# Attention in a four-layer kernel: the order of three matmul groups in a round, the sum of the weights on one engine, the division in four parts

## The chip, the cores and the metric

The kernel runs on one NeuronCore of a Trainium2 chip. The engines that matter here are TensorE (PE in the profile; PEld is its weight load), VectorE (DVE), ScalarE (ACT) and GpSimd (POOL). Matmuls write to PSUM, eight banks of 512 float32 columns on 128 partitions; GpSimd works on SBUF only. The metric is the device time of one execution in microseconds, and the median of the runs is what counts.

## The reference, cut to what matters

Four layers, each followed by a residual sum and a layer norm, on 2048 tokens of 128 numbers: a test-time-training attention, an 8-expert feed-forward layer, a softmax attention, and a gated 8-expert layer. The change is in the third:

```python
q = (x @ Wq).reshape(b, s, 16, 64)      # s = 2048 tokens, 16 heads of 64
k = (x @ Wk).reshape(b, s, 16, 64)
v = (x @ Wv).reshape(b, s, 16, 64)
dot = jnp.einsum('bihd,bkhd->bhik', q, k)
w = jax.nn.softmax(dot / 8, axis=-1)
a = jnp.einsum('bhij,bjhd->bihd', w, v).reshape(b, s, 1024)
return a @ Wo + bo
```

## The kernel before, in words

The attention goes through 32 units. A unit U is a pair of heads (p = U // 4) and 512 queries (U % 4); head h of the pair lies on rows 64h to 64h+63 of every operand. A unit has 8 rounds (d = 0 to 7, R = 8U + d), and a round covers two steps, that is two blocks of 128 keys. There are 256 rounds.

What TensorE does in one round, in the order of its queue (loop at L1827):

1. **late maximum** (`maximum`, L1734 to L1742, matmuls at L1740): two matmuls, one for each head, with 64 rows each, into banks 5 and 6. They are rough scores of unit U+1 (U+2 from d = 7 on), of 128 queries against 512 keys, and serve only to find each query's maximum. DVE reduces the two banks (L1945) and gives them back through the semaphore `free5`. There is no second pair of banks for this.
2. **the negated maxima** (L1758 to L1760): four matmuls with 32 rows each that write minus the maximum into the four score banks 0 to 3. They wait until ACT has taken the exponentials of the round before (L1757).
3. **scores** (L1761 to L1767): twelve matmuls with 64 rows, two by two (six pairs), added to the same four banks.
4. **early maximum** (L1740 again): like the late one, for the next 128 queries. It waits at L1699 until DVE has given banks 5 and 6 back after the late one.
5. at most one **misc job** in bank 7 (`misc_job`, L1568): keys at d = 0, the output product of unit U-2 at d = 1, the sum of the weights of U-1 over the partitions at d = 2, values at d = 3, queries at d = 4, the negated maxima turned by a matmul (`mask`, L1744) at d = 7.
6. **weigh** (L1769 to L1783): eight matmuls with 128 rows and 64 columns, the values times the exponentials of the round before, into bank 4.

ACT takes two exponentials a round (L1883, 128x1024 each), written to eight buffers `Pb`. The sum over the keys is kept in `acc`: `acc += Pb` for 15 of a unit's 16 steps, columns 0 to 831 on GpSimd (L2077) and 832 to 1023 on DVE (L1996). ACT reuses a buffer when weigh and both adds of eight steps ago are done.

DVE's queue in a round (L2024 to L2043): reduce of the late maximum, `negate` at d = 7 (L1947, two small reduces after all maxima of the next unit), the two adds of the round before, reduce of the early maximum, its part of the misc job, one quarter of the reciprocal of the sum at d = 3 to 6 (`invert`, L1968), and at d = 7 the product of reciprocal and head output (`normalise`, L1976, 128x512).

Semaphores order all of this; the queues are written out by hand and `Plan` (L1593) only numbers the uses of each bank.

Of the kernel before, what the change touches and what calls it, by code (L numbers as in the profile page):

```python
# [16 lines left out]
P = 128  # L17
# [52 lines left out]
NT = 16  # L70
# [1488 lines left out]
RN = NT // 2  # L1559
ROUNDS = UNITS * RN  # L1560
STEPS = 2 * ROUNDS
POOL = 832
BUFS = 8
SCALE = 1.0 / float(np.sqrt(D))
B_O, B_M, B_P = 4, 5, 7
# [2 lines left out]
def misc_job(R):  # L1568

    U, d = R // RN, R % RN  # L1570
    p, qt = U // NU, U % NU
    if d == 0 and p < PAIRS - 1:
        return "k", p + 1, qt
    if d == 1 and U > 1:
        return "out", U - 2
    if d == 2 and U:
        return "sum", U - 1
    if d == 3 and p // 2 < PAIRS // 2 - 1:
        return "v", p // 2 + 1, U % RN
    if d == 4 and U < UNITS - 2:  # L1580
        return "q", U + 2
    if d == 7 and U < UNITS - 1:
        return "mask", U + 1
    return None
# [107 lines left out]
def attention_pe(k):  # L1692
# [12 lines left out]
    def freed(key):  # L1705
        bank, n = plan.at[key]
        pe.wait_ge(S[f"free{bank}"], n)
# [38 lines left out]
        bank = begin(("mask", U))  # L1746
        end(pe.matmul(ps[:, bank, 0:P], b.nm[:, :], k.ident[:, :], start=True, stop=True), bank)

    def scores(R):
        U, d = R // RN, R % RN  # L1750
        p = U // NU
        if d == 0:
            freed(("mask", U))
            freed(("q", U))
            freed(("k", p, NU - 1))
        if R:
            pe.wait_ge(S["probs"], 2 * R)  # L1757
        for g in range(4):  # L1758
            rows = slice(32 * g, 32 * (g + 1))
            pe.matmul(ps[:, 2 * (g % 2) + g // 2, :], b.ones[rows, :], b.Mr[rows, :], start=True, stop=False, tile_position=(32 * g, 0))  # L1760
        for i in range(2):  # L1761
            kc, slot = 2 * d + i, 2 * i
            at = slice(kc * P, (kc + 1) * P)
            for n, (K, Q) in enumerate(((b.Kh, b.Qh), (b.Kh, b.Ql), (b.Kl, b.Qh))):
                for h in range(2):
                    last = pe.matmul(ps[:, slot + h, :], K[HEAD[h], p % 2, at], Q[HEAD[h], U % 3, :], start=False, stop=(n == 2))  # L1766
            last.then_inc(S["scores"], 1)  # L1767
# [15 lines left out]
            last.then_inc(S["weighted"], 1)  # L1783

    def sums(U):
        pe.wait_ge(S["added_dve"], 15 * (U + 1))
        pe.wait_ge(S["added_pool"], 15 * (U + 1))
        bank = begin(("sum", U))
        for h in range(2):
            last = pe.matmul(ps[HEAD[h], bank, :], k.ones[:, 0:D], b.acc[:, U % 2, h * QT:(h + 1) * QT], start=True, stop=True)  # L1790
        end(last, bank)

    def output(U):
        pe.wait_ge(S["normalised"], U + 1)
        bank = begin(("out", U))
        end(pe.matmul(ps[:, bank, :], k.att_o[:, U // NU, :], b.On[:, :], start=True, stop=True), bank)  # L1796

# [28 lines left out]
    pe.wait_ge(S["att_wo"], 16)  # L1826
    for R in range(ROUNDS):  # L1827
        late, early = max_jobs(R - 1)[1], max_jobs(R)[0]
        if R and late:
            maximum(*late[1:])  # L1830
        scores(R)
        if early:
            maximum(*early[1:])
        if misc_job(R):
            misc(misc_job(R))
        if R:
            weigh(R - 1)
# [11 lines left out]
def attention_act(k):  # L1849
    b, S, ps, act = k.a, k.S, k.ps, k.nc.scalar  # L1850
    plan = b.plan

    def begin(key):
        bank, n = plan.at[key]
        act.wait_ge(S[f"full{bank}"], n)
        return bank

    def queries(U):
        bank = begin(("q", U))
        act.activation(b.Qh[:, U % 3, :], ps[:, bank, :], ACT.Copy).then_inc(S["high"], 1)  # L1860

    def keys(p, qt):
        bank = begin(("k", p, qt))
        act.activation(b.Kh[:, p % 2, qt * QT:(qt + 1) * QT], ps[:, bank, :], ACT.Copy).then_inc(S["high"], 1)

    def values(G, j):
        bank = begin(("v", G, j))
        act.activation(b.Vb[:, G % 2, 2 * j:2 * j + 2, :].rearrange("p a d -> p (a d)"), ps[:, bank, :], ACT.Copy).then_inc(S[f"free{bank}"], 1)

    def sums(U):  # L1870
        bank = begin(("sum", U))
        if U:
            act.wait_ge(S["inverted"], 4 * U)
        act.activation(b.ssum[:, :], ps[:, bank, :], ACT.Copy).then_inc(S[f"free{bank}"], 1)  # L1874

    def probs(step):
        slot = 2 * (step % 2)
        act.wait_ge(S["scores"], step + 1)
        if step >= BUFS:
            act.wait_ge(S["weighted"], step - BUFS + 1)  # L1880
            act.wait_ge(S["added_dve"], adds_of(step - BUFS))
            act.wait_ge(S["added_pool"], adds_of(step - BUFS))
        act.activation(b.Pb[:, step % BUFS, :], ps[:, slot:slot + 2, :].rearrange("p a b -> p (a b)"), ACT.Exp, scale=SCALE).then_inc(S["probs"], 1)  # L1883

    def heads_out(U):
        act.wait_ge(S["weighted"], NT * (U + 1))
        if U > 1:
            act.wait_ge(S["normalised"], U - 1)
        act.activation(b.Or[:, U % 2, :], ps[:, B_O, :], ACT.Copy).then_inc(S["heads_out"], 1)

    act.wait_ge(S["tile_y0"], 16 * (SLOTS_T // 2))
    act.wait_ge(S["tile_y1"], 16 * (SLOTS_T // 2))
    act.activation(b.ones[:, :], k.ones[:, :], ACT.Copy)
    gather_norm_act(k, 1)
    for g in range(NU):
        bank = begin(("x", g))
        act.activation(b.xh[:, g * QT:(g + 1) * QT], ps[:, bank, :], ACT.Copy).then_inc(S["high"], 1)
    queries(0)
    for qt in range(NU):
        keys(0, qt)  # L1900
    queries(1)
    for j in range(RN):
        values(0, j)
    for R in range(ROUNDS):
        U, d = R // RN, R % RN
        probs(2 * R)
        probs(2 * R + 1)
        key = misc_job(R)
        if key and key[0] in "qkv":
            {"q": queries, "k": keys, "v": values}[key[0]](*key[1:])  # L1910
        if key and key[0] == "sum":
            sums(U - 1)
        if d == 0 and U:
            heads_out(U - 1)
    heads_out(UNITS - 1)
    sums(UNITS - 1)
    for g in range(4):
        norm_act(k, 8 + g, g)


def attention_dve(k):
# [20 lines left out]
    def maximum(U, m):  # L1942
        quarter, qc = m // 4, m % 4
        bank = begin(("max", U, m))
        v.tensor_reduce(b.mx[:, :, qc, quarter:quarter + 1], ps[:, bank:bank + 2, :], AX.X, ALU.max).then_inc(S[f"free{bank}"], 1)  # L1945

    def negate(U):  # L1947
# [14 lines left out]
                        ALU.mult).then_inc(S[f"free{bank}"], 1)  # L1962

    def invert(U, part):
        bank, n = plan.at["sum", U]
        v.wait_ge(S[f"free{bank}"], n)
        at = slice(part * P, (part + 1) * P)
        v.reciprocal(b.rec[:, at], b.ssum[:, at]).then_inc(S["inverted"], 1)  # L1968

    def normalise(U):  # L1970
        v.wait_ge(S["inverted"], 4 * U + 4)
        v.wait_ge(S["heads_out"], U + 1)
        if U:
            bank, n = plan.at["out", U - 1]
            v.wait_ge(S[f"full{bank}"], n)
        v.tensor_tensor(b.On[:, :], b.rec[:, :], b.Or[:, U % 2, :], ALU.mult).then_inc(S["normalised"], 1)  # L1976

    def output(U):
        qt = U % NU
# [2 lines left out]
            v.wait_ge(S[f"free{bank}"], plan.at["out", U - NU][1])  # L1982
        yq = k.y_all[:, 4 * qt:4 * qt + 4, :]
        v.tensor_tensor(yq, ps[:, bank, :].rearrange("p (a d) -> p a d", a=4), yq, ALU.add).then_inc(S[f"free{bank}"], 1)

    def add(step):
        U, kc = step // NT, step % NT
        u, at = U % 2, slice(POOL, 2 * QT)
        v.wait_ge(S["probs"], step + 1)
        if kc > 1:  # L1990
            v.wait_ge(S["added_dve"], adds_of(step - 1))
        elif U > 1:
            bank, n = plan.at["sum", U - 2]
            v.wait_ge(S[f"full{bank}"], n)
        before = b.Pb[:, (step - 1) % BUFS, at] if kc == 1 else b.acc[:, u, at]
        v.tensor_tensor(b.acc[:, u, at], before, b.Pb[:, step % BUFS, at], ALU.add).then_inc(S["added_dve"], 1)  # L1996

    v.wait_ge(S["tile_y0"], 16 * (SLOTS_T // 2))
    v.wait_ge(S["tile_y1"], 16 * (SLOTS_T // 2))
# [24 lines left out]
    for R in range(ROUNDS):  # L2024
# [3 lines left out]
            maximum(*late[1:])  # L2028
        if d == 7 and U < UNITS - 1:
            negate(U + 1)  # L2030
        if R:
            if (R - 1) % RN:
                add(2 * R - 2)
            add(2 * R - 1)
        if early:
            maximum(*early[1:])
        key = misc_job(R)
        if key and key[0] in ("q", "k", "mask", "out"):
            {"q": queries, "k": keys, "mask": mask, "out": output}[key[0]](*key[1:])
        if U and 3 <= d <= 6:  # L2040
            invert(U - 1, d - 3)
        if U and d == 7:
            normalise(U - 1)  # L2043
    for step in (STEPS - 2, STEPS - 1):
        add(step)
    output(UNITS - 2)
    for part in range(4):
        invert(UNITS - 1, part)
    normalise(UNITS - 1)
    output(UNITS - 1)  # L2050


# [10 lines left out]
def attention_pool(k):  # L2063
# [2 lines left out]

    def add(step):
        U, kc = step // NT, step % NT
        u, at = U % 2, slice(0, POOL)
        g.wait_ge(S["probs"], step + 1)  # L2070
        if kc == 1 and U > 1:
            bank, n = plan.at["sum", U - 2]
            g.wait_ge(S[f"full{bank}"], n)
        if step > 1:
            g.wait_ge(S["added_pool"], adds_of(step - 1) if kc > 1 else 15 * U)
        before = b.Pb[:, (step - 1) % BUFS, at] if kc == 1 else b.acc[:, u, at]
        g.tensor_tensor(b.acc[:, u, at], before, b.Pb[:, step % BUFS, at], ALU.add).then_inc(S["added_pool"], 1)  # L2077

    for step in range(STEPS):
        if step % NT:  # L2080
# [78 lines left out]
```

## Time and profile before

| | us |
|---|---|
| three timed runs | 1982.34, 1986.2, 1986.29 |
| median | 1986.2 |
| the profiled execution | 1982.01 |
| its span, first to last instruction | 1980.3 |
| attention rounds in it | from 474.4 to about 1786 |
| PE busy | 1745.4 (88%) |
| DVE busy | 1392.0 (70%) |
| POOL busy | 1095.0 (55%) |
| ACT busy | 792.9 (40%) |

A busy share is the time an engine had an instruction in flight, and a busy PE is not PE at its peak, since matmuls overlap one another. What tells more is the distance from one group of matmuls to the next. Start and duration stand in microseconds in timeline rows, and rows there may merge several equal instructions (x2, x4).

### The profile page before, as it was taken

What the parts mean: (1) busy time and instruction counts of PE and PEld (TensorE: products, weight loads), DVE (VectorE), ACT (ScalarE), POOL (GpSimd) and SP (SyncE); (2) the same over time, 40 slices, a digit from 0 to 9 for tenths busy, and PEclk for the clock granted to TensorE, in tenths of its full rate; (3) what the DMA queues carried; (4) which work ended last, traced back from release to release, by engine and by line L of the source; (5) the groups of instructions that cost most, each with busy time, mean ns of one, the idle gap of its engine ahead of it and who ended that gap; (6) DMA issues with size and microseconds to landing.
All of it is one profiled execution on the core that took longest, in us unless ns stands there. A gap on an engine that the chain in (4) does not pass through costs nothing.

```text
span 1980.3 us, 35242 instructions
## 1 busy us (share of the span) xinstructions
PE 1745.4 (88%) x13630; PEld 948.8 (48%) x13630; DVE 1392.0 (70%) x2440; ACT 792.9 (40%) x1181; POOL 1095.0 (55%) x644
## 2 busy tenths in 40 slices
PE   4888751948999999999999999999999999995893
PEld 3666641834444444444444444444444444443482
DVE  3666654347787777887777877778778887786474
ACT  3444420533444444444444444444444444441131
POOL 2232204032777677776767767777677777682303
PEclk8886755969999999999999999999999999996897
DMA  7000000210000000000000000000000000003122
GB/s 243 4 3 3 3 1 30 62 38 1 1 1 1 1 1 1 1 1 1 1 1 1 1 1 1 1 1 1 1 1 1 1 1 1 1 1 99 32 58 60
DMA packets 41533, 32.76 MB, mean 17 GB/s; under 512 B 3604, under 2 KB 37392, under 8 KB 41368
## 3 DMA queue, kind: packets, MB, share of 16 engines
q1 hardware_dynamic: 31096, 22.12, 3.6%
q0 software_dynamic: 2048, 4.20, 0.7%
q10 hardware_dynamic: 8224, 4.19, 0.7%
q8 instruction: 110, 1.80, 0.4%
q14 instruction: 55, 0.45, 0.1%
HBM read 18.96 MB, written 11.53 MB: 15 GB/s over the span
## 4 chain that ended last, share of the span: by engine, by line
PE 81%; DVE 9%; issue 5%; POOL 3%; ACT 1%; DMA 1%; SPq 0%; DVEq 0%; POOLq 0%; ACTq 0%
PE psum L1781 23%; PE psum L1766 20%; PE psum L1740 8%; PE psum L1760 6%; PE psum L1407 2%; PE psum L1796 2%; PE psum L1790 2%; PE psum L1181 1%; PE psum L1713 1%; PE psum L1193 1%; PE psum L1367 1%; DVE a_mx L1945 1%; POOL a_acc L2077 1%; PE psum L1417 1%; PE psum L447 1%
## 5 line engine op out<-in xcount | busy, mean ns | idle before, releaser
L2077 POOL TENSOR_TENSOR a_acc<-a_acc,a_Pb 128x832 f32<-128x832 f32 x448 | 893.3, 1994 | 307.8 <-ACT a_Pb L1883 275.1
L1945 DVE TENSOR_REDUCE a_mx<-psum 128x2 f32<-128x1024 f32 x512 | 625.5, 1224 | 237.2 <-PE psum L1740 234.2
L1883 ACT ACTIVATE a_Pb<-psum 128x1024 f32<-128x1024 f32 x512 | 496.7, 1022 | 703.5 <-PE psum L1766 701.5
L1781 PE MATMUL psum<-a_Pb,a_Vb 128*64 128x512 f32 x2048 | 494.3, 604 | 0.0
L1996 DVE TENSOR_TENSOR a_acc<-a_acc,a_Pb 128x192 f32<-128x192 f32 x448 | 230.9, 515 | 28.9 <-ACT a_Pb L1883 5.4
L1781 PEld LDWEIGHTS psum<-a_Pb,a_Vb 128*64 128x64 f32 x2048 | 127.2, 136 | 244.7 <-issue 173.7
L1740 PE MATMUL psum<-a_Kh,a_Qh 64*128 64x512 f32 x1024 | 231.3, 447 | 8.4 <-DVE a_mx L1945 8.3
L1766 PE MATMUL psum<-a_Qh,a_Kh 64*128 64x512 f32 x1024 | 231.1, 447 | 0.0
L1766 PE MATMUL psum<-a_Ql,a_Kh 64*128 64x512 f32 x1024 | 203.8, 393 | 0.0
L1740 PEld LDWEIGHTS psum<-a_Kh,a_Qh 64*128 64x128 f32 x1024 | 97.1, 184 | 222.6 <-issue 211.6
L1766 PE MATMUL psum<-a_Qh,a_Kl 64*128 64x512 f32 x1024 | 203.4, 392 | 0.0
L1766 PEld LDWEIGHTS psum<-a_Qh,a_Kh 64*128 64x128 f32 x1024 | 96.8, 185 | 74.4 <-issue 62.7
L1760 PE MATMUL psum<-a_Mr,a_ones_r 32*128 32x512 f32 x1024 | 129.8, 496 | 0.0
L1968 DVE RECIPROCAL a_rec<-a_ssum 128x128 f32<-128x128 f32 x128 | 120.3, 942 | 3.9 <-ACT a_ssum L1874 3.9
L2077 POOL TENSOR_TENSOR a_acc<-a_Pb 128x832 f32<-128x832 f32 x32 | 62.9, 1965 | 91.4 <-ACT a_Pb L1883 91.4
L1766 PEld LDWEIGHTS psum<-a_Qh,a_Kl 64*128 64x128 f32 x1024 | 97.8, 186 | 22.5
L1766 PEld LDWEIGHTS psum<-a_Ql,a_Kh 64*128 64x128 f32 x1024 | 97.7, 187 | 11.3
L1760 PEld LDWEIGHTS psum<-a_Mr,a_ones_r 32*128 32x128 f32 x1024 | 49.1, 182 | 67.4 <-issue 62.3
L786 POOL TENSOR_TENSOR t_gq<-t_gq,t_sigq 128x512 f32<-128x512 f32 x7 | 8.8, 1264 | 116.6 <-ACT t_sigq L503 116.6
L969 POOL DMA_INDIRECT g_xg<-y_rows,slots x16 | 15.1, 947 | 100.4 <-DMA y_rows<-g_tile_y 95.8
L960 POOL DMA_INDIRECT x_rows<-x_all,slots x16 | 15.6, 972 | 74.5 <-issue 74.5
L969 POOL DMA_INDIRECT y_all<-y_rows,slots x16 | 15.2, 951 | 73.4 <-issue 73.4
(385 smaller groups left out, 2004.0 us busy)
## 6 DMA issues: line engine op xcount, KB each, us to landing
x_rows<-zero ACTq DMA_DIRECT2D x2, 2048.0 KB, 20.9
g_w<-in_L_ffn_w_eDF_dram SPq DMA_DIRECT2D x2, 1408.0 KB, 8.7
r_W<-in_L_ffn_W_dram SPq DMA_DIRECT2D x1, 2048.0 KB, 12.4
r_tile_x<-x_rows SPq DMA_DIRECT2D x16, 128.0 KB, 2.1
y_rows<-r_tile_y SPq DMA_DIRECT2D x16, 128.0 KB, 1.8
g_tile_x<-x_rows SPq DMA_DIRECT2D x16, 128.0 KB, 2.2
y_rows<-g_tile_y SPq DMA_DIRECT2D x16, 128.0 KB, 1.8
g_w<-in_L_ffn_w_eFD_dram SPq DMA_DIRECT2D x2, 512.0 KB, 10.5
```

The source lines that it names most:

```text
L1407: last = pe.matmul(hp[:, at:at + TILE], b.w13s[:, u, j // FC1, (j % FC1) * P:(j % FC1 + 1) * P], b.xT[:, u, :], start=True, stop=True)
L1740: last = pe.matmul(ps[:, bank + h, :], b.Qh[HEAD[h], U % 3, qc * P:(qc + 1) * P], b.Kh[HEAD[h], p % 2, quarter * QT:(quarter + 1) * QT], s ...
L1760: pe.matmul(ps[:, 2 * (g % 2) + g // 2, :], b.ones[rows, :], b.Mr[rows, :], start=True, stop=False, tile_position=(32 * g, 0))
L1766: last = pe.matmul(ps[:, slot + h, :], K[HEAD[h], p % 2, at], Q[HEAD[h], U % 3, :], start=False, stop=(n == 2))
L1781: last = pe.matmul(ps[HEAD[h], B_O, :], b.Vb[:, p // 2 % 2, kc, at], b.Pb[:, step % BUFS, h * QT:(h + 1) * QT], start=(kc == 0), stop=(kc ...
L1790: last = pe.matmul(ps[HEAD[h], bank, :], k.ones[:, 0:D], b.acc[:, U % 2, h * QT:(h + 1) * QT], start=True, stop=True)
L1796: end(pe.matmul(ps[:, bank, :], k.att_o[:, U // NU, :], b.On[:, :], start=True, stop=True), bank)
L1883: act.activation(b.Pb[:, step % BUFS, :], ps[:, slot:slot + 2, :].rearrange("p a b -> p (a b)"), ACT.Exp, scale=SCALE).then_inc(S["probs"], 1)
L1945: v.tensor_reduce(b.mx[:, :, qc, quarter:quarter + 1], ps[:, bank:bank + 2, :], AX.X, ALU.max).then_inc(S[f"free{bank}"], 1)
L1968: v.reciprocal(b.rec[:, at], b.ssum[:, at]).then_inc(S["inverted"], 1)
L1996: v.tensor_tensor(b.acc[:, u, at], before, b.Pb[:, step % BUFS, at], ALU.add).then_inc(S["added_dve"], 1)
L2077: g.tensor_tensor(b.acc[:, u, at], before, b.Pb[:, step % BUFS, at], ALU.add).then_inc(S["added_pool"], 1)
```

## The change

Three edits.

- On TensorE the four matmuls of the negated maxima become a function of their own, `less_maxima`, which now opens a round: negated maxima, late maximum, scores, early maximum, misc job, weigh. The waits for the exponentials and for the mask go with it.
- DVE's adds are removed; GpSimd adds all 1024 columns. `added` takes the place of `added_dve` and `added_pool`.
- The division: the sum moves from d = 2 to d = 1 and the output product from d = 1 to d = 2. DVE inverts at d = 2 to 5, now ahead of the early maximum's reduce, and normalises in four parts of 128 columns at d = 3, 5, 6 and 7, after its misc job; after the last unit inversion and product alternate. The waits that keep `rec` and `nm` from being overwritten are written out (two `wait_ge` on DVE for its own earlier work).

```diff
-    if d == 1 and U > 1:
-        return "out", U - 2
-    if d == 2 and U:
-        return "sum", U - 1
+    if d == 1 and U:
+        return "sum", U - 1
+    if d == 2 and U > 1:
+        return "out", U - 2
...
-    def scores(R):
+    def less_maxima(R):
         U, d = R // RN, R % RN
-        p = U // NU
         if d == 0:
             freed(("mask", U))
-            freed(("q", U))
-            freed(("k", p, NU - 1))
         if R:
             pe.wait_ge(S["probs"], 2 * R)
         for g in range(4):
             rows = slice(32 * g, 32 * (g + 1))
             pe.matmul(ps[:, 2 * (g % 2) + g // 2, :], b.ones[rows, :], b.Mr[rows, :], start=True, stop=False, tile_position=(32 * g, 0))
+
+    def scores(R):
...
     for R in range(ROUNDS):
         late, early = max_jobs(R - 1)[1], max_jobs(R)[0]
+        less_maxima(R)
         if R and late:
             maximum(*late[1:])
         scores(R)
...
         quarter, qc = m // 4, m % 4
         bank = begin(("max", U, m))
+        if U and m == 0:
+            v.wait_ge(S["negated"], U)
...
-    def normalise(U):
-        v.wait_ge(S["inverted"], 4 * U + 4)
+    def normalise(U, part):
+        v.wait_ge(S["inverted"], 4 * U + part + 1)
...
-        v.tensor_tensor(b.On[:, :], b.rec[:, :], b.Or[:, U % 2, :], ALU.mult).then_inc(S["normalised"], 1)
+        at = slice(part * P, (part + 1) * P)
+        v.tensor_tensor(b.On[:, at], b.rec[:, at], b.Or[:, U % 2, at], ALU.mult).then_inc(S["normalised"], 1)
...
-        if R:
-            if (R - 1) % RN:
-                add(2 * R - 2)
-            add(2 * R - 1)
+        if U and 2 <= d <= 5:
+            invert(U - 1, d - 2)
         if early:
             maximum(*early[1:])
...
-        if U and 3 <= d <= 6:
-            invert(U - 1, d - 3)
-        if U and d == 7:
-            normalise(U - 1)
-    for step in (STEPS - 2, STEPS - 1):
-        add(step)
+        if U and d in (3, 5, 6, 7):
+            normalise(U - 1, (3, 5, 6, 7).index(d))
     output(UNITS - 2)
     for part in range(4):
         invert(UNITS - 1, part)
-    normalise(UNITS - 1)
+        normalise(UNITS - 1, part)
...
-        before = b.Pb[:, (step - 1) % BUFS, at] if kc == 1 else b.acc[:, u, at]
-        g.tensor_tensor(b.acc[:, u, at], before, b.Pb[:, step % BUFS, at], ALU.add).then_inc(S["added_pool"], 1)
+        before = b.Pb[:, (step - 1) % BUFS, :] if kc == 1 else b.acc[:, u, :]
+        g.tensor_tensor(b.acc[:, u, :], before, b.Pb[:, step % BUFS, :], ALU.add).then_inc(S["added"], 1)
```

## Rows read from the trace of the kernel before

**Rows 1.** Page parts 1 and 4, then busy time by engine over the rounds.

```profile
PE 1745.4 (88%) x13630; PEld 948.8 (48%) x13630; DVE 1392.0 (70%) x2440; ACT 792.9 (40%) x1181; POOL 1095.0 (55%) x644
...
PE 81%; DVE 9%; issue 5%; POOL 3%; ACT 1%; DMA 1%; SPq 0%; DVEq 0%; POOLq 0%; ACTq 0%
...
474.00:1783.00 1309.00, 1305.20 (x7672) 611.41 (x7670) 1022.62 (x1308) 571.73 (x654) 948.53 (x477) 1.00 0.00 1
```

**Rows 2.** Timeline of PE, one round without misc job: start, duration, instruction.

```profile
917.59 0.50 PE L1740 MATMUL psum<-a_Kh,a_Qh 64*128 64x512 f32 x2
918.02 0.51 PE L1760 MATMUL psum<-a_Mr,a_ones_r 32*128 32x512 f32 x4
918.47 0.50 PE L1766 MATMUL psum<-a_Qh,a_Kh 64*128 64x512 f32 x2
918.81 0.40 PE L1766 MATMUL psum<-a_Ql,a_Kh 64*128 64x512 f32 x2
...
919.98 0.40 PE L1740 MATMUL psum<-a_Kh,a_Qh 64*128 64x512 f32 x2
920.30 1.94 PE L1781 MATMUL psum<-a_Pb,a_Vb 128*64 128x512 f32 x8
922.17 0.50 PE L1740 MATMUL psum<-a_Kh,a_Qh 64*128 64x512 f32 x2
```

**Rows 3.** The same round on DVE and ACT.

```profile
918.14 1.23 DVE L1945 TENSOR_REDUCE a_mx<-psum 128x2 f32<-128x1024 f32 x1 [0.21 <-PE psum L1740]
919.28 1.03 DVE L1996 TENSOR_TENSOR a_acc<-a_acc,a_Pb 128x192 f32<-128x192 f32 x1
920.69 1.22 DVE L1945 TENSOR_REDUCE a_mx<-psum 128x2 f32<-128x1024 f32 x1
...
919.48 1.94 ACT L1883 ACTIVATE a_Pb<-psum 128x1024 f32<-128x1024 f32 x2 [2.63 <-PE psum L1766]
```

**Rows 4.** Before the rounds: a PE pair that waited for DVE's reduce.

```profile
452.08 1.22 DVE L1945 TENSOR_REDUCE a_mx<-psum 128x2 f32<-128x1024 f32 x1
...
453.44 0.51 PE L1740 MATMUL psum<-a_Kh,a_Qh 64*128 64x512 f32 x2 [0.63 <-DVE a_mx L1945]
453.88 0.39 PE L1729 MATMUL psum<-att_Wvh,a_xh 128*128 128x256 f32 x1
```

**Rows 5.** PE in the last unit, whose rounds have no maxima.

```profile
1772.88 1.94 PE L1781 MATMUL psum<-a_Pb,a_Vb 128*64 128x512 f32 x8
1774.74 0.51 PE L1760 MATMUL psum<-a_Mr,a_ones_r 32*128 32x512 f32 x4
```

**Rows 6.** What `negate` (L1956) takes and waits for: min/median/max ns; then us, times.

```profile
L1956 DVE TENSOR_REDUCE a_nm<-a_mx x64: 174/181/188, 470.4 to 1750.7; 128x8 f32<-128x32 f32 x64
...
  DVE a_mx L1945: 6.7, 31
```

**Rows 7.** GpSimd's adds, one of 1024 columns elsewhere, and the last unit.

```profile
L2077 POOL TENSOR_TENSOR a_acc<-a_acc,a_Pb x448: 1935/1964/2486, 482.3 to 1789.2; 128x832 f32<-128x832 f32 x150
...
L1686 POOL TENSOR_TENSOR att_Wkl<-att_raw,att_Wkh x1: 2341/2341/2341, 342.2 to 342.2; 128x1024 fp32r<-128x1024 f32 x1
...
916.01 4.08 POOL L2077 TENSOR_TENSOR a_acc<-a_acc,a_Pb 128x832 f32<-128x832 f32 x2 [1.38 <-ACT a_Pb L1883]
...
1759.81 1.95 POOL L2077 TENSOR_TENSOR a_acc<-a_acc,a_Pb 128x832 f32<-128x832 f32 x1 [0.84 <-ACT a_Pb L1883]
1780.23 10.88 POOL L2077 TENSOR_TENSOR a_acc<-a_acc,a_Pb 128x832 f32<-128x832 f32 x5
```

**Rows 8.** DVE's adds and division: min/median/max ns; the last reciprocals and product.

```profile
L1996 DVE TENSOR_TENSOR a_acc<-a_acc,a_Pb x448: 341/358/2121, 485.6 to 1787.3; 128x192 f32<-128x192 f32 x150
L1976 DVE TENSOR_TENSOR a_On<-a_rec,a_Or x32: 679/719/2245, 553.8 to 1797.3; 128x512 f32<-128x512 f32 x32
L1968 DVE RECIPROCAL a_rec<-a_ssum x128: 894/943/953, 532.8 to 1796.3; 128x128 f32<-128x128 f32 x128
...
1793.85 3.39 DVE L1968 RECIPROCAL a_rec<-a_ssum 128x128 f32<-128x128 f32 x4 [3.85 <-ACT a_ssum L1874]
```

More of the change, by code:

```diff
@@ L1561 @@
 STEPS = 2 * ROUNDS
-POOL = 832
 BUFS = 8
@@ L1760, in scores @@
             pe.matmul(ps[:, 2 * (g % 2) + g // 2, :], b.ones[rows, :], b.Mr[rows, :], start=True, stop=False, tile_position=(32 * g, 0))
+    def scores(R):
+        U, d = R // RN, R % RN
+        p = U // NU
+        if d == 0:
+            freed(("q", U))
+            freed(("k", p, NU - 1))
         for i in range(2):
@@ L1785, in sums @@
     def sums(U):
-        pe.wait_ge(S["added_dve"], 15 * (U + 1))
-        pe.wait_ge(S["added_pool"], 15 * (U + 1))
+        pe.wait_ge(S["added"], 15 * (U + 1))
         bank = begin(("sum", U))
@@ L1793, in output @@
     def output(U):
-        pe.wait_ge(S["normalised"], U + 1)
+        pe.wait_ge(S["normalised"], 4 * U + 4)
         bank = begin(("out", U))
@@ L1880, in probs @@
             act.wait_ge(S["weighted"], step - BUFS + 1)
-            act.wait_ge(S["added_dve"], adds_of(step - BUFS))
-            act.wait_ge(S["added_pool"], adds_of(step - BUFS))
+            act.wait_ge(S["added"], adds_of(step - BUFS))
         act.activation(b.Pb[:, step % BUFS, :], ps[:, slot:slot + 2, :].rearrange("p a b -> p (a b)"), ACT.Exp, scale=SCALE).then_inc(S["probs"], 1)
@@ L1887, in heads_out @@
         if U > 1:
-            act.wait_ge(S["normalised"], U - 1)
+            act.wait_ge(S["normalised"], 4 * U - 4)
         act.activation(b.Or[:, U % 2, :], ps[:, B_O, :], ACT.Copy).then_inc(S["heads_out"], 1)
@@ L1964, in invert @@
     def invert(U, part):
+        if U and part == 0:
+            v.wait_ge(S["normalised"], 4 * U)
         bank, n = plan.at["sum", U]
@@ L1968, in invert @@
         v.reciprocal(b.rec[:, at], b.ssum[:, at]).then_inc(S["inverted"], 1)
-    def normalise(U):
-        v.wait_ge(S["inverted"], 4 * U + 4)
+    def normalise(U, part):
+        v.wait_ge(S["inverted"], 4 * U + part + 1)
         v.wait_ge(S["heads_out"], U + 1)
-        if U:
+        if U and part == 0:
             bank, n = plan.at["out", U - 1]
             v.wait_ge(S[f"full{bank}"], n)
-        v.tensor_tensor(b.On[:, :], b.rec[:, :], b.Or[:, U % 2, :], ALU.mult).then_inc(S["normalised"], 1)
+        at = slice(part * P, (part + 1) * P)
+        v.tensor_tensor(b.On[:, at], b.rec[:, at], b.Or[:, U % 2, at], ALU.mult).then_inc(S["normalised"], 1)
     def output(U):
@@ L1984, in output @@
         v.tensor_tensor(yq, ps[:, bank, :].rearrange("p (a d) -> p a d", a=4), yq, ALU.add).then_inc(S[f"free{bank}"], 1)
[L1986 to L1994, printed above, removed]
-        before = b.Pb[:, (step - 1) % BUFS, at] if kc == 1 else b.acc[:, u, at]
-        v.tensor_tensor(b.acc[:, u, at], before, b.Pb[:, step % BUFS, at], ALU.add).then_inc(S["added_dve"], 1)
     v.wait_ge(S["tile_y0"], 16 * (SLOTS_T // 2))
@@ L2068, in add @@
         U, kc = step // NT, step % NT
-        u, at = U % 2, slice(0, POOL)
+        u = U % 2
         g.wait_ge(S["probs"], step + 1)
@@ L2074, in add @@
         if step > 1:
-            g.wait_ge(S["added_pool"], adds_of(step - 1) if kc > 1 else 15 * U)
-        before = b.Pb[:, (step - 1) % BUFS, at] if kc == 1 else b.acc[:, u, at]
-        g.tensor_tensor(b.acc[:, u, at], before, b.Pb[:, step % BUFS, at], ALU.add).then_inc(S["added_pool"], 1)
+            g.wait_ge(S["added"], adds_of(step - 1) if kc > 1 else 15 * U)
+        before = b.Pb[:, (step - 1) % BUFS, :] if kc == 1 else b.acc[:, u, :]
+        g.tensor_tensor(b.acc[:, u, :], before, b.Pb[:, step % BUFS, :], ALU.add).then_inc(S["added"], 1)
     for step in range(STEPS):
```

## The prediction

> **What bounds the kernel now.** I read the page's busy line first, then the chain that ended last, then busy time over the rounds alone [rows 1]. PE is busy 88% of the span, but what the reader is to see is the last row: between 474 and 1783 us PE is busy 1305.2 of 1309.0, and the chain lies 81% on PE. The attention's rounds are PE's own queue, 256 rounds in 1309 us or 5.11 each, and nothing else sets their pace. Busy time doesn't say what in the queue costs, because matmuls overlap; the timeline does, as distances between the starts of groups [rows 2]. In the round shown: late maximum to negated maxima 0.43, these to the first pair of scores 0.45, first to second pair 0.34, then five distances of 0.23 (918.81 to 919.98), early maximum to weigh 0.32, weigh to the next round 1.87. Sum 4.58. The same two maximum matmuls thus cost 0.43 alone between groups of another shape, and 0.23 where they follow pairs of their own shape (64x128). The first pair after a change of shape costs 0.10 more than one in a run, and the last before a change 0.09 more.
>
> The second thing to read is how banks 5 and 6 go round [rows 3]. Late maximum starts at 917.59, DVE's reduce at 918.14 (0.55 later) and takes 1.23, to 919.37. The early maximum starts at 919.98, so it has 0.61 to spare. DVE's load is no bound, but this loop is nearly one: the order before puts 2.39 us between late and early, 2.19 between early and late.
>
> **The change, part by part.**
>
> *The order.* Saved: 0.43 + 0.45 + 0.34 become 0.45 (negated maxima to the late pair, again 32 rows to 64), 0.34 (late pair, now first of its run) and 0.24 (first scores, now second). That is 1.22 against 1.03, 0.19 to 0.20 a round. Weigh to the negated maxima costs what weigh to the late maximum did: 1.86 in the last unit, which has no maxima [rows 5]. There are 247 rounds with a late maximum: 0.195 x 247 = 48 us to be had.
>
> But late and early now stand with only the scores between them. Left alone, the early pair would start 0.34 + 0.24 + 1.17 (918.81 to 919.98) = 1.75 after the late one. Its banks are free only after 0.545 + 1.226 = 1.77 [rows 3], and PE needs time on top. That price stands before the rounds, where PE did wait for this reduce [rows 4]: DVE ends at 453.30, the pair starts at 453.44 and the group after it at 453.88, 0.58 after DVE's end (0.57 in the rows that repeat it; I take 0.575). That beats adding 0.14 to 1.77, since a pair that finds the array empty keeps its follower waiting 0.44, not 0.32. So late pair to the group behind the early one becomes 1.77 + 0.575 = 2.35, where 1.75 + 0.32 = 2.07 was wanted: a stall of 0.28 in each of the 246 rounds that have both. Net 0.28 - 0.195 = 0.085 a round, and 0.085 x 246 = **20.9 us more**. A round like [rows 2] goes from 4.58 to 0.45 + 2.35 + 1.87 = 4.66. Bounds: no stall at all gives -48; a stall of 0.17 (pair starts at 1.92 instead of 1.75, no later cost) gives about -6; a stall of 0.28 with half the saving gives +45.
>
> The negated maxima now open the round and still wait for both exponentials. ACT's two end 2.95 after the first scores (918.47 to 919.48 + 1.94 = 921.42) [rows 2, 3], that is 3.64 after the round's start in the new order (0.45 + 0.34 + 2.95, less 0.10 for the shorter distance to the second pair); the next round starts at 4.66. Cover 1.0, cost nothing; behind them in PE's queue stands everything. The mask at d = 7 waits for `negate`, which waits for the late reduce: 0.22 of waiting and 0.28 for the two reduces of 0.18 that overlap [rows 6], 0.50 after the reduce's end, and the mask's matmul would start 0.575 after it. Just covered; 0 taken, up to 0.1 x 31 = 3 us otherwise.
>
> *GpSimd alone.* DVE loses its adds, 448 of them with a median of 0.36 [rows 8], that lay between its reduces; DVE isn't on the path, so nothing is saved on PE. An add on GpSimd goes from 1.96 for 832 columns to 2.34 for 1024, by the row of a two-input instruction of that size; I take 2.36. Two in a row cost 4.08, so 0.14 between them [rows 7]: 2.50 each, 15 in a unit 37.5 of a unit's 41.5 (5.11 + 0.085, eight times). It keeps up; it would set the pace only from 2.77. The eight buffers cover four rounds, so ACT's wait eight steps back is not reached.
>
> In the last unit it isn't covered. Rounds without maxima are 4.58 - 0.43 - 0.23 = 3.9, two adds take 5.0. Before, GpSimd's second add there started at 1759.81, when its exponential came, and the last ended at 1780.23 + 10.88 = 1791.11 [rows 7], with the sums right after. From the same start 14 adds of 2.50 end at 1794.8: **3.7 us more**. (Bounds: 0, and 6 with adds of 2.6.)
>
> *Sum and output product swapped, reciprocals earlier.* The sum at d = 1 needs GpSimd's last add of the unit before; by GpSimd's pace this ends some 3.5 us into d = 0, and the sum's turn comes at about 8 us. The reciprocals of 0.94 [rows 8] stand between DVE's late and early reduce at d = 2 to 5: late reduce ends 2.22 into the round, reciprocal 3.17, early reduce 4.4 instead of 4.1, and the next late maximum needs its banks at 4.66 + 0.45. Covered. In the tail the last four alternate with products: 3.39 + 0.69 becomes about 4 x (0.85 + 0.28 + 0.04) = 4.6, **0.5 us more**.
>
> *Four products.* A part of 128 columns costs DVE about 0.28 (0.68 for 512, 0.35 for 192). DVE has the room; but see the second rival for what it can wait for.
>
> Sum: 20.9 - 0.2 (the one late maximum without an early one) + 3.7 + 0.5 = 24.9, say 25, on the profiled execution's own 1982.0 (span 1980.3 and 1.7 around it): **2007 us**. The median shown is 1986.2, 4.2 above that execution; the runs scatter by that much, so I keep 2007 and let the range hold the rest.
>
> **The rivals.**
>
> *A: the saving arrives in full.* If the reduce didn't hold the early pair, 48 us go and 4.2 come: 1938. For it: the distances of [rows 2] are the same in round after round, and the last unit's run shows the same costs at a change of shape. Against it: 1.77 is more than 1.75 even before PE's reaction, and there is one pair of banks. TensorEngine Tiling (Array Packing) in the Trainium skill, Key Properties, says that changing the tiling mode, not just the tile, drains TensorE. [...] Chance 0.10.
>
> *B: GpSimd blocks DVE, and DVE blocks PE.* A DVE product has two inputs in SBUF, as its adds had. The add issued at 919.28 while GpSimd's ran to 916.01 + 4.08 = 920.09 took 1.03 instead of 0.36 and ended at 920.31; the longest took 2.1, and the product's longest 2.2 [rows 3, 7, 8]. So it waits for the end of GpSimd's add. GpSimd now runs 90% of the time. The exponentials end 2.7 and 3.6 into a round. At d = 5, the first round of 4.66, GpSimd starts at 2.8, then at 5.3 and 7.8, which is 3.1 into d = 6, and that add ends at 5.5. The part issued there at 4.1 ends at 5.6, which is 0.96 into d = 7, and the late reduce is due at 0.99. The part of d = 7 ends about 0.1 ahead of its reduce. At these two places there is no reserve; if adds come 0.5 later than my count, each unit loses 2 x 0.5 us: 31 x 1.0 = 31 more, 2038. It decides from adds of about 2.4, against my 2.36. The Trainium skill, SBUF — State Buffer, Who interferes with whom, gives the rule: a DVE instruction with two SBUF inputs contends with a GpSimd instruction that reads SBUF, and the loser blocks fully. The trace agrees, by the row at 919.28. Chance 0.13.
>
> *C: the stall is the smaller one* (0.17 to 0.20), so that loss and saving cancel and about the tail is left: 1980 to 1987. For it: a pair that comes only a little late may not find the array empty. Chance 0.07.
>
> *D: the saving doesn't come, only the stall:* 0.28 x 246 + 4 = 73, 2055. Against it: the 0.23 of the early pair. Chance 0.05.
>
> **How the numbers follow.** The main case has 0.65 and a range of its own from 1998 to 2016. For this kernel 0.2% is 4 us, about what a measurement can tell from no change. Slower: main, B and D, 0.83; faster: A and a fifth or so of C, 0.12; the same: 0.05. The range leaves A and D out and takes in the near side of C and most of B: 1986 to 2034.
>
> **What would show it.** On PE's timeline: negated maxima, 0.45, late pair, then seven starts in one run at 0.34, 0.24 and 0.23, and then the early pair starting about 1.92 (not 1.75) after the late one, its follower 0.44 later; PE's waits on the reduce of L1945 in nearly every round. A round without misc job at 4.66. If the late to early distance reads 1.75, the main step is wrong. GpSimd's mean near 2.36 and ACT never waiting for it; products of 128 columns up to 2.5 us long, and a late reduce that starts over 1.0 into d = 7 or d = 0 is rival B. The last unit about 4 us longer from its second add to the output.

## The result, and the profile after

The changed kernel takes 2007.89 us (median of four runs, 2001.3 to 2010.29), the kernel before 1984.9 in the same comparison (four runs, 1982.34 to 1986.29). The ratio is 1.0106, with a 95% interval of 1.0085 to 1.0126: slower by 1.1%. The forecast was 2007, and slower.

The page of the changed kernel: busy time by engine, and the costliest groups (line, engine, operation, shapes, count, then busy us and mean ns, then idle time before them and what ended it).

```profile
PE 1769.4 (88%) x13630; PEld 962.9 (48%) x13630; DVE 1305.7 (65%) x2056; ACT 801.9 (40%) x1181; POOL 1279.2 (64%) x644
...
L2066 POOL TENSOR_TENSOR a_acc<-a_acc,a_Pb 128x1024 f32<-128x1024 f32 x448 | 1064.5, 2376 | 183.3 <-ACT a_Pb L1885 139.7
...
L1739 PE MATMUL psum<-a_Kh,a_Qh 64*128 64x512 f32 x1024 | 256.3, 490 | 11.8 <-DVE a_mx L1949 5.3
...
L1983 DVE TENSOR_TENSOR a_On<-a_rec,a_Or 128x128 f32<-128x128 f32 x128 | 174.6, 1365 | 0.1
```

By [rows 1], DVE lost 86 us of work and GpSimd took on 184; neither says why the kernel is slower. Nor does the idle time: the page puts 5.3 us on waits for DVE's reduce. A pair of a run lasts 0.39 and its successor is due 0.23 after its start, so a pair that comes 0.2 late finds its predecessor only just done, and PE looks idle for some 0.03 (by the median; 7 us over all rounds). The stall stands in the distances. PE's timeline of the changed kernel, a round without misc job, as in [rows 2]:

```profile
890.81 0.51 PE L1756 MATMUL psum<-a_Mr,a_ones_r 32*128 32x512 f32 x4
891.25 0.50 PE L1739 MATMUL psum<-a_Kh,a_Qh 64*128 64x512 f32 x2
891.59 0.40 PE L1769 MATMUL psum<-a_Qh,a_Kh 64*128 64x512 f32 x2
891.83 0.39 PE L1769 MATMUL psum<-a_Ql,a_Kh 64*128 64x512 f32 x2
...
892.74 0.39 PE L1769 MATMUL psum<-a_Qh,a_Kl 64*128 64x512 f32 x2
893.17 0.51 PE L1739 MATMUL psum<-a_Kh,a_Qh 64*128 64x512 f32 x2
893.60 1.94 PE L1784 MATMUL psum<-a_Pb,a_Vb 128*64 128x512 f32 x8
895.47 0.51 PE L1756 MATMUL psum<-a_Mr,a_ones_r 32*128 32x512 f32 x4
```

The run of seven is there (0.34, then 0.24 and 0.23). The early pair starts 1.92 after the late one and 0.43 after the pair before it, where 0.23 is the pace; its follower comes 0.43 later instead of 0.32. The round takes 4.66. DVE in the same stretch:

```profile
891.79 1.23 DVE L1949 TENSOR_REDUCE a_mx<-psum 128x2 f32<-128x1024 f32 x1 [0.32 <-PE psum L1739]
893.71 1.23 DVE L1949 TENSOR_REDUCE a_mx<-psum 128x2 f32<-128x1024 f32 x1 [0.69 <-PE psum L1739]
894.85 1.67 DVE L1983 TENSOR_TENSOR a_On<-a_rec,a_Or 128x128 f32<-128x128 f32 x1
896.45 1.23 DVE L1949 TENSOR_REDUCE a_mx<-psum 128x2 f32<-128x1024 f32 x1
```

The reduce ends at 893.02 and the early pair starts 0.15 later. The third line is a product held by GpSimd, whose add ends at about 896.4: its row ends at 896.52, just as the late reduce of d = 7 is due, 0.98 into its round.

For all that follows I measure a unit: from one d = 0's negated maxima to the next's, median of 31. It is 41.47 before and 42.21 after (the first two units and the last seven have fewer misc jobs and are shorter). The spans of the profiled executions, 1980.3 and 2009.0, differ by 28.7: the rounds begin 7.7 later (482.1 against 474.4 us, in code that is the same in both), 31 units take 1296.1 against 1279.0, and what follows, the last unit and the code behind it, takes 3.9 more. The 17.1 hide 6.4 by which three units of the kernel before were too long. In two of its rounds PE waited 1.38 and 1.80 us for DVE (under order_only below), 3.2 together; and behind each wait the clock was granted at 1.2 instead of 2.4 GHz for a stretch, which is the rest (columns: stretch, length, busy time of PE, PEld, DVE, ACT, POOL, then granted clock):

```profile
1013.10:1016.40 3.30, 3.30 (x15) 2.15 (x11) 2.31 (x4) 2.05 (x2) 0.31 (x1) 0.50 0.00 0
1709.40:1712.70 3.30, 3.30 (x16) 2.12 (x14) 2.15 (x6) 2.05 (x2) 1.50 (x1) 0.50 0.00 0
```

By the unit it is 0.745 x 31 = 23 us in the 31 units and 3.9 behind them.

### The profile page after: what moved, and what is told of

The parts are those of the page before. It is cut to its first block, busy times and chain, and to the rows that moved or that the text cites. A ratio compares the mean times of both kernels' runs of the same rounds, so it can differ in the third digit from the quotient of the medians.

```text
span 2009.0 us, 34034 instructions
## 1 busy us (share of the span) xinstructions
PE 1769.4 (88%) x13630; PEld 962.9 (48%) x13630; DVE 1305.7 (65%) x2056; ACT 801.9 (40%) x1181; POOL 1279.2 (64%) x644
## 4 chain that ended last, share of the span: by engine, by line
PE 80%; DVE 9%; issue 5%; POOL 3%; DMA 1%; ACT 1%; SPq 0%; another core or an unknown queue 0%; DVEq 0%; POOLq 0%; ACTq 0%
PE psum L1784 23%; PE psum L1769 17%; PE psum L1739 11%; PE psum L1756 5%; PE psum L1407 2%; PE psum L1798 2%; PE psum L1792 2%; PE psum L1181 1%; PE psum L1712 1%; DVE a_mx L1949 1%; PE psum L1193 1%; PE psum L1417 1%; PE psum L447 1%; PE psum L452 1%; PE psum L349 1%
## 5 line engine op out<-in xcount | busy, mean ns | idle before, releaser
L2066 POOL TENSOR_TENSOR a_acc<-a_acc,a_Pb 128x1024 f32<-128x1024 f32 x448 | 1064.5, 2376 | 183.3 <-ACT a_Pb L1885 139.7
L1949 DVE TENSOR_REDUCE a_mx<-psum 128x2 f32<-128x1024 f32 x512 | 618.7, 1211 | 340.8 <-PE psum L1739 340.7
L1739 PE MATMUL psum<-a_Kh,a_Qh 64*128 64x512 f32 x1024 | 256.3, 490 | 11.8 <-DVE a_mx L1949 5.3
L1769 PE MATMUL psum<-a_Qh,a_Kh 64*128 64x512 f32 x1024 | 204.3, 393 | 0.0
L1739 PEld LDWEIGHTS psum<-a_Kh,a_Qh 64*128 64x128 f32 x1024 | 102.8, 183 | 175.0 <-issue 173.6
L1983 DVE TENSOR_TENSOR a_On<-a_rec,a_Or 128x128 f32<-128x128 f32 x128 | 174.6, 1365 | 0.1
L2066 POOL TENSOR_TENSOR a_acc<-a_Pb 128x1024 f32<-128x1024 f32 x32 | 75.8, 2367 | 52.7 <-ACT a_Pb L1885 52.6
```

The source lines that it names most:

```text
L1739: last = pe.matmul(ps[:, bank + h, :], b.Qh[HEAD[h], U % 3, qc * P:(qc + 1) * P], b.Kh[HEAD[h], p % 2, quarter * QT:(quarter + 1) * QT], s ...
L1983: v.tensor_tensor(b.On[:, at], b.rec[:, at], b.Or[:, U % 2, at], ALU.mult).then_inc(S["normalised"], 1)
L2066: g.tensor_tensor(b.acc[:, u, :], before, b.Pb[:, step % BUFS, :], ALU.add).then_inc(S["added"], 1)
```

## The experiments

| kernel | median us | median of before beside it | ratio, 95% interval | unit |
|---|---|---|---|---|
| order_only | 2072.34 | 1984.7 | 1.0442, 1.0417 to 1.0468 | 43.93 |
| rest_only | 1999.63 | 1984.7 | 1.0075, 1.0052 to 1.0099 | 41.97 |
| three_quarters | 1968.81 | 1984.7 | 0.991, 0.988 to 0.994 | 40.81 |
| split_after | 1953.94 | 1984.7 | 0.9849, 0.9823 to 0.9875 | 40.53 |
| rest_moved | 1984.55 | 1981.64 | 1.0018, 1.0002 to 1.0033 | 41.45 |
| after_moved | 2011.74 | 1981.64 | 1.0163, 1.0136 to 1.0189 | 42.40 |
| split_moved | 1934.24 | 1981.64 | 0.9765, 0.9731 to 0.98 | 39.99 |
| split_last | 1926.22 | 1981.64 | 0.9721, 0.9694 to 0.9748 | 39.99 |

**order_only: the order without the rest.**

```diff
+        less_maxima(R)
         if R and late:
             maximum(*late[1:])
         scores(R)
```

> The kernel before with one edit: the negated maxima open the round, the late maximum follows. GpSimd's and DVE's adds and the division stay as before. Main theory (the early pair waits for DVE's reduce of the late one): distance late to early pair 1.92 instead of 1.75, a round without misc job 4.65, 246 x 0.085 = 21 us slower, about 2005 against 1985. Rival 'GpSimd': the loss comes from the longer adds and the blocked products, then this kernel shows the saving alone, about 1937. Rival 'tail only': within 4 us of before.

The stall came as expected (late to early 1.91, rounds of 4.65), and the kernel lost 88 us, not 21. What I left out is DVE's queue behind `negate`. Timeline of order_only at d = 7:

```profile
1049.63 0.35 DVE L2001 TENSOR_TENSOR a_acc<-a_acc,a_Pb 128x192 f32<-128x192 f32 x1
1049.81 4.07 POOL L2082 TENSOR_TENSOR a_acc<-a_acc,a_Pb 128x832 f32<-128x832 f32 x2 [0.56 <-ACT a_Pb L1888]
...
1050.45 1.55 DVE L2001 TENSOR_TENSOR a_acc<-a_acc,a_Pb 128x192 f32<-128x192 f32 x1 [0.47 <-DVE a_acc L2001]
1051.93 1.21 DVE L1950 TENSOR_REDUCE a_mx<-psum 128x2 f32<-128x1024 f32 x1
1053.06 0.67 DVE L1966 TENSOR_TENSOR a_Mr<-psum,a_mask 128x512 fp32r<-128x512 f32 x1
...
1053.79 0.51 PE L1757 MATMUL psum<-a_Mr,a_ones_r 32*128 32x512 f32 x4 [1.62 <-DVE a_Mr L1966]
```

`negate` comes 0.44 later than before, with the late reduce. The second add now starts behind GpSimd's (0.64 in these rows, 0.28 by the median of the units) and waits for its end; the early reduce, the mask's product and so the negated maxima that open the next round stand behind it, and PE waits 1.62 us once a unit. So the removal of DVE's adds, which I priced at nothing, is worth some 1.7 us a unit once the order is changed: d = 7 takes 6.76 here and 5.07 in the changed kernel. It is the order's condition. This is read from the rows; no run removes the adds alone.

The kernel before was close to the same fault. At d = 7 its second add starts 0.11 ahead of GpSimd's by the median and takes 0.36. In unit 12 it came 0.26 behind. Timeline of before:

```profile
1008.08 4.04 POOL L2077 TENSOR_TENSOR a_acc<-a_acc,a_Pb 128x832 f32<-128x832 f32 x2 [0.42 <-ACT a_Pb L1883]
...
1008.34 1.91 DVE L1996 TENSOR_TENSOR a_acc<-a_acc,a_Pb 128x192 f32<-128x192 f32 x1 [0.47 <-ACT a_Pb L1883]
...
1010.17 1.21 DVE L1945 TENSOR_REDUCE a_mx<-psum 128x2 f32<-128x1024 f32 x1
...
1011.53 0.50 PE L1740 MATMUL psum<-a_Kh,a_Qh 64*128 64x512 f32 x2 [1.38 <-DVE a_mx L1945]
```

The add held the early reduce, and the reduce held the next late maximum. The same happened once more, at 1704.71, with a wait of 1.80. What made the add late in these two rounds is not shown.

**rest_only: the rest without the order.**

```diff
-        less_maxima(R)
         if R and late:
             maximum(*late[1:])
+        less_maxima(R)
         scores(R)
```

> The changed kernel with the old order of the queue (late maximum, negated maxima, scores); all the rest of the change stays. Main theory: rounds as before (4.55 to 4.58 without misc job), only the tail is longer by 4 us, 1989 against 1985. Rival 'GpSimd': 2003 or more, late reduces that start late behind products of up to 2.5 us.

1999.6: 15 us more than before, not 4, and in the rounds most of it at d = 7 (5.41 instead of 4.98 by the median). This is the rival with GpSimd. Timeline of rest_only around the start of d = 7:

```profile
1054.22 7.38 POOL L2066 TENSOR_TENSOR a_acc<-a_acc,a_Pb 128x1024 f32<-128x1024 f32 x3
1054.71 2.02 DVE L1983 TENSOR_TENSOR a_On<-a_rec,a_Or 128x128 f32<-128x128 f32 x1
1055.33 0.49 PE L1739 MATMUL psum<-a_Kh,a_Qh 64*128 64x512 f32 x2
...
1056.66 1.21 DVE L1949 TENSOR_REDUCE a_mx<-psum 128x2 f32<-128x1024 f32 x1
...
1058.01 0.50 PE L1739 MATMUL psum<-a_Kh,a_Qh 64*128 64x512 f32 x2 [0.17 <-DVE a_mx L1949]
```

The product, 0.28 by itself, takes 2.02 until GpSimd's add ends; the late reduce starts 1.33 after its pair instead of 0.55, and the early pair and the mask wait for it.

**three_quarters: a shorter reduce.**

```diff
-        v.tensor_reduce(..., ps[:, bank:bank + 2, :], AX.X, ALU.max)
+        v.tensor_reduce(..., ps[:, bank:bank + 2, 0:384 if U and m % 2 else 512], AX.X, ALU.max)
```

> The changed kernel; DVE's reduce of the late maximum reads 384 of 512 columns of each bank, so a quarter of those keys is left out of the search for the maxima. The reduce goes from 1.23 to about 0.96 us. Main theory: banks are back 0.545 + 0.96 = 1.50 after the late pair, follower possible at 2.08 where 2.07 is wanted, so the stall of 0.28 is gone and the full saving stands: rounds without misc job at 4.38, about 0.28 x 246 = 69 us less than the changed kernel, 1939. Rival 'the stall is not the reduce' (exponentials, GpSimd, drain): 2008 as before this edit.

With a reduce of 0.96 the early pair starts on time and the follower is at 0.36. PE's timeline of three_quarters, d = 1:

```profile
890.60 0.51 PE L1756 MATMUL psum<-a_Mr,a_ones_r 32*128 32x512 f32 x4
891.03 0.50 PE L1739 MATMUL psum<-a_Kh,a_Qh 64*128 64x512 f32 x2
...
892.76 0.43 PE L1739 MATMUL psum<-a_Kh,a_Qh 64*128 64x512 f32 x2
893.12 1.08 PE L1792 MATMUL psum<-a_acc,ones 128*64 128x512 f32 x4
```

Late to early 1.73, rounds without misc job 4.38. So the stall is the reduce. But 39 us went, not 69: d = 7 takes 5.32 where the changed kernel takes 5.07, and its late reduce starts 1.51 into the round, held by a product; the one of d = 0 starts at 1.22, and that round gained only 0.05. The time that the stall had given the products is gone too.

**split_after: the same without leaving anything out.** ACT copies the second bank while DVE reduces the first.

```diff
+            act.activation(b.mc[:, 0, :], ps[:, B_M + 1, :], ACT.Copy).then_inc(S["max_copied"], 1)
         probs(2 * R)
...
+        v.tensor_reduce(b.mx[:, 0:1, ...], ps[:, bank:bank + 1, :], AX.X, ALU.max).then_inc(S[f"free{bank}"], 1)
+        v.wait_ge(S["max_copied"], R)
+        v.tensor_reduce(b.mx[:, 1:2, ...], b.mc[:, :, :], AX.X, ALU.max).then_inc(S["max_reduced"], 1)
```

> The changed kernel; ACT copies the late maximum's second bank (512 columns, 0.60 us) to SBUF while DVE reduces the first (about 0.7), and DVE reduces the copy afterwards; the early pair waits for these two alone. Nothing of the computation is left out. Main theory: both banks are back about 1.25 after the late pair, no stall, rounds of 4.38, less 69 us; at d = 7 negate comes behind two reduces of 0.69 and the mask's matmul waits 0.37 more, 31 x 0.37 = 11 back: about 1950. Rival 'exponentials': ACT's copy comes ahead of them in its queue and delays them, 0.3 or more a round, so less than half of the gain. Rival 'stall is not the reduce': no gain.

1953.9 for 1950: late to early 1.72, rounds of 4.35, the exponentials not delayed (they start 1.67 and 2.6 into the round, as in the changed kernel). But d = 7 was again held by a product: its late reduce starts at 1.58 and the round takes 5.51 by the median (5.35, which the next expectations use, is the mean).

**rest_moved and after_moved: the products out of the way.** Parts 0 and 1 at d = 3 and 4, parts 2 and 3 at d = 0 and 1 of the next unit.

```diff
+        if U > 1 and d < 2:
+            normalise(U - 2, 2 + d)
+        if U and d in (3, 4):
+            normalise(U - 1, d - 3)
         key = misc_job(R)
...
-        if U and d in (3, 5, 6, 7):
-            normalise(U - 1, (3, 5, 6, 7).index(d))
```

> The changed kernel in the old order (as rest_only), and DVE's products moved: parts 0 and 1 of a unit at d = 3 and 4, parts 2 and 3 at d = 0 and 1 of the next unit, ahead of the misc job; none is left at d = 5, 6 and 7. Theory now (the 15 us of rest_only are products that wait for GpSimd's adds at d = 6 and hold up the late reduce of d = 7, on which negate and the mask wait): d = 7 back from 5.38 to 4.98, a unit from 41.97 to 41.47, 14 to 16 us less than rest_only, about 1988. Rival (GpSimd's pace itself, adds of 2.37 in place of 1.96, costs the 0.5 a unit): d = 7 and the unit stay as in rest_only, 2000.

> The changed kernel with the same move of the products (d = 3, 4, and 0, 1 of the next unit). Theory: in the changed kernel the products end just in time and cost nothing, so the rounds stay: 4.65 without misc job, 5.07 at d = 7, a unit 42.22, and 2008 within 4. Rival (part of the loss is blocked products): 5 to 15 us less.

rest_moved: d = 7 back at 4.98, the unit at 41.45, 1984.6. That is 15 us below rest_only, or 12 if each is taken against the before beside it; the 31 units of the profiled executions differ by 12.4. What is left, 1.8 parts in a thousand above before, fits the tail: in the profiled executions what follows the 31 units is 5.5 longer than before. So GpSimd's longer adds cost the rounds next to nothing (units of 41.45 to 41.55, for 41.47); the products did. after_moved: most rounds unchanged, as expected, but the unit is 0.19 longer and the median 2011.7: the part at d = 0 now held the misc job's product and with it the late reduce of d = 1, so that round took 5.69 instead of 5.50. Timeline of DVE in after_moved:

```profile
893.83 2.18 DVE L1983 TENSOR_TENSOR a_On<-a_rec,a_Or 128x128 f32<-128x128 f32 x1
895.93 0.68 DVE L1935 TENSOR_TENSOR a_Kl<-psum,a_Kh 128x512 fp32r<-128x512 f32 x1
896.53 1.21 DVE L1949 TENSOR_REDUCE a_mx<-psum 128x2 f32<-128x1024 f32 x1
```

The same move of an instruction is worth 12 to 15 us in one kernel and costs about 6 in the other (0.19 x 31): what counts is where GpSimd's adds stand when it is issued.

**split_moved and split_last.** The split with the moved products, and then DVE alone adding in the last unit, where it has nothing else to do.

```diff
-    for step in range(STEPS):
+    for step in range(STEPS - NT):
         if step % NT:
             add(step)
```

> split_after with the same move of the products. There the late reduce of d = 7 started 1.59 into the round instead of 0.98 and that round took 5.35. Theory: it starts at 0.98 again, d = 7 falls to 5.0 (mask behind two reduces, negate), the unit from 40.53 to about 40.1, 12 us less than split_after: 1942. Rival (GpSimd at 15 x 2.52 = 37.8 of 40 is the pace): no change, 1954.

> split_moved, and in the last unit, whose rounds have no maxima, DVE alone adds the weights (1024 columns, about 1.2 us) in place of GpSimd (2.38 and 0.14 between). Theory: GpSimd's adds set the end of the last unit; with DVE's the last sum follows the last exponential by some 1.5 us instead of 7: 5 us less than split_moved, 1937. Rival (the tail is set by the sums and the division alone): within 1 us of split_moved.

Both beat the kernel before: 1934.2 and 1926.2 (for 1942 and 1937), against 1981.6; the changed kernel takes 2007.9 against its 1984.9. d = 7 takes 4.95, the unit 39.99. The timeline of PE, ACT and DVE in split_last, d = 6:

```profile
868.62 0.50 PE L1757 MATMUL psum<-a_Mr,a_ones_r 32*128 32x512 f32 x4
869.06 0.50 PE L1740 MATMUL psum<-a_Kh,a_Qh 64*128 64x512 f32 x2
...
869.60 0.60 ACT L1916 ACTIVATE a_mc<-psum 128x512 f32<-128x512 f32 x1 [1.71 <-PE psum L1740]
869.60 0.69 DVE L1963 TENSOR_REDUCE a_mx<-psum 128x1 f32<-128x512 f32 x1 [1.09 <-PE psum L1740]
...
870.76 0.40 PE L1740 MATMUL psum<-a_Kh,a_Qh 64*128 64x512 f32 x2
871.09 1.94 PE L1785 MATMUL psum<-a_Pb,a_Vb 128*64 128x512 f32 x8
...
872.96 0.51 PE L1757 MATMUL psum<-a_Mr,a_ones_r 32*128 32x512 f32 x4
```

The banks are back by 870.29, early starts at 870.76, the round is 4.34. Behind the 31 units the profiled execution took 225.6 us, against 230.0 in split_moved and 227.0 before.

## Why the prediction was right, step by step

- *The saving of the order*, 0.195 a round, is real: 4.34 to 4.38 where the stall is gone (four kernels), against 4.55 to 4.58. That is what rival A said, and it was wrong in total because the early pair then came too soon for its banks. The rule behind it (the Trainium skill, TensorEngine Tiling (Array Packing), Key Properties: a change of tiling mode drains the array) agrees in its sign with these kernels. The page gives no size; the 0.20 is measured here alone.
- *The stall*, 0.28 a round: shown. 1.92 and 0.43 were forecast as 1.92 and 0.44, and it goes when the reduce is shortened or split. Net 0.093 a round (0.745 / 8) where I had 0.085: 23 us for 20.9. The exponentials are not the cause: they end 3.61 into the round with the stall and without it, well ahead of the next negated maxima.
- *GpSimd alone*: adds of 2.376 mean, for 2.36. It keeps up, and the last one ends 3.8 later in its unit than before, for 3.7. Changing who adds in the last unit took 4.4 us off what follows the rounds (8 by the medians). *The division in the tail*: 4.84 against 4.11, 0.7 for 0.5 (four steps of 1.17 are 4.68 and not 4.6, so 0.6 was due). The whole part behind the 31 units grew by 3.9, for 4.2. It belongs to these two edits and not to the order: it is 226.5 in order_only, 227.0 before, and 230.0 to 233.9 in every kernel in which GpSimd alone adds up to the end.
- *Rival B, no reserve*: the products were held until GpSimd's add ended (mean 1.365 us for 0.28), and in the changed kernel cost nothing: the late reduce starts 0.97 or 0.98 into the round in every d by the median. This was the narrow step, and luck had a part in it. I had the part of d = 6 end 0.96 into d = 7, and by the median its row ends at 1.03; the part of d = 7 ends at 1.00, not 0.1 ahead of its reduce. The reduce could start at 0.98 only because the rows of DVE's instructions overlap by 0.07 to 0.09 when they follow one another (918.14 + 1.23 = 919.37, the next at 919.28). A reserve of 0.02 to 0.04 was left. rest_only shows the price, 0.5 us a unit, where the products meet GpSimd's adds at another time. My range ended at 2034 and so left out rival B's own 2038, though I wrote that it took in most of B. By the rule of the Trainium skill (SBUF — State Buffer, Who interferes with whom) the port pair that DVE shares with GpSimd is an exclusive lock; the trace agrees, by the 2.02 us of that product.
- *What was too simple*: I took the edits as terms of a sum. They aren't. Order alone is +88 us, the rest alone +15, both together +23. DVE's adds, which I had put off the path, were off it by 0.11 us before, and not in two of its rounds; they are on it once the late reduce comes 0.44 later. The total was right because I followed the new schedule for the whole change; my expectations for the parts alone, which I worked out as differences, missed by 67 and 11 us. That 2007 and 2007.89 lie within 1 us is luck: the traces give 23 + 3.9 = 27 for my 25, the kernel before lost 6.4 in its own trace, and the four runs of the changed kernel spread over 9 us.
- *Rivals C and D* fall with the rows of 1.92 and 0.43, and with the rounds of 4.34.

Left open: what made the rounds begin between 469 and 482 us in different executions; that part is the same code everywhere. It and the short stretches of lower clock may make most of the scatter between executions; only one execution of each kernel has a trace, so this is not shown.

## What to carry to other kernels

Where a PSUM bank has a single copy, add up the loop through it (matmul to reduce 0.55, reduce 1.23, reaction 0.15, and a restart of the array worth 0.1 more) before moving either of its matmuls: a cheaper place for one can bring it closer to its partner than the loop allows. Such a stall hardly shows as idle time; look for a distance of 0.43 in a run of 0.23. If a bank must come back sooner, share its evacuation between two engines. And an instruction that another engine can hold (the longest product of the changed kernel took 2.47 us for 0.28) must not stand ahead of one with a due time.

## What I had not expected of the hardware

In order_only the granted clock fell to 1.2 GHz again and again during the rounds, in thirteen stretches of some 3.4 us (one of them below, columns as above). They lie whole units apart, as PE's waits for the mask do, and each began less than 2 us after such a wait had ended (1.6 us long, once 3.4). Only 13 of 30 such waits were followed by one; what decides is not shown. The scores' distances went from 0.23 to 0.43, and such a unit took 1.2 us more than its neighbours (45.1 against 43.9). The two stretches of the kernel before came in the same way, behind waits of 1.38 and 1.80 us. In the rounds of the other eight kernels PE never waited more than 0.8 us, and their clock did not fall there, in the changed kernel and its 0.28 a round neither.

```profile
917.30:920.60 3.30, 3.30 (x15) 2.16 (x12) 2.25 (x4) 1.85 (x2) 0.00 (x0) 0.50 0.02 5
```
